# A decoder's product-key memory stage: masking in one operation, 1/Z on the one-hots, another order of work

## The reference

```python
q = (xn @ w_q.T).reshape(b, n, 2, h, kd).transpose(2, 0, 1, 3, 4)      # h = 8 heads
sim = jnp.einsum('pbnhd,hkpd->pbnhk', q, keys)                         # 2 sides x 8 heads x 32 keys
s, i = jax.lax.top_k(sim, k)                                           # k = 8
all_scores = (sx[..., :, None] + sy[..., None, :]).reshape(b, n, h, k * k)
scores, pk = jax.lax.top_k(all_scores, k)
w_down, w_up = key_in[idx], key_out[idx]                               # of 1024 experts
o = jnp.einsum('bnd,bnhkd->bnhk', inputs, w_down)
o = jax.nn.gelu(o, approximate=False) * jax.nn.softmax(scores, axis=-1)
return jnp.einsum('bnhk,bnhkd->bnd', o, w_up)
```

## Time and profile before

| | |
|---|---|
| median of 3 runs | 2909.44 us (2908.89 to 2909.66) |
| profiled execution | 2916.36 us, span 2914.3 us |
| TensorE busy | 2524.5 us (87%) |
| VectorE busy | 2382.4 us (82%) |
| ScalarE busy | 1835.6 us (63%) |
| GpSimd busy | 1101.8 us (38%) |
| mean granted TensorE clock | 0.926 of full speed |
| memory stage | from about 650 to 1433 us, 64 tiles |

### The profile page before, as it was taken

How to read it: one execution, slowest core, us unless ns; L and a number is a source line. 1 busy time by engine, 2 the same in 40 slices (tenths; PEclk the granted TensorE clock), 3 DMA queues, 4 the chain that set the end, 5 groups by cost and what they waited for, 6 DMA issues and landing times.

```text
span 2914.3 us, 95817 instructions
## 1 busy us (share of the span) xinstructions
PE 2524.5 (87%) x35786; PEld 1958.3 (67%) x35786; DVE 2382.4 (82%) x6431; ACT 1835.6 (63%) x3307; POOL 1101.8 (38%) x981
## 2 busy tenths in 40 slices
PE   2999963867888888888799999877789999999999
PEld 2666642546777777777566666555577888888887
DVE  6999989687899999999599999677767777777776
ACT  1777763544566666666366666565666777777776
POOL 1444420008899999999323232344413000000000
PEclk9999985977999999999799999798969999999999
DMA  5000000000000000000100000000001111111111
GB/s 165 1 0 0 0 15 0 1 0 2 1 0 0 0 0 0 0 0 0 59 1 0 0 0 0 9 15 16 14 5 52 51 55 51 54 51 54 55 53 48
DMA packets 47578, 60.44 MB, mean 21 GB/s; under 512 B 6672, under 2 KB 25872, under 8 KB 47376
## 3 DMA queue, kind: packets, MB, share of 16 engines
q1 hardware_dynamic: 47504, 59.45, 6.7%
HBM read 54.98 MB, written 4.46 MB: 20 GB/s over the span
## 4 chain that ended last, share of the span: by engine, by line
PE 77%; DVE 13%; issue 6%; DVEq 2%; ACT 1%; POOL 1%; DMA 0%; ACTq 0%; POOLq 0%; SPq 0%
PE ps L1064 8%; PE ps L885 8%; PE ps L1053 5%; PE ps L912 4%; PE ps L927 4%; PE ps L1078 4%; PE ps L1155 4%; PE ps L1133 4%; PE ps L1157 4%; PE ps L1156 4%; PE ps L1135 4%; PE ps L1134 4%; DVE work L1587 3%; DVE work L1636 2%; PE ps L940 2%
## 5 line engine op out<-in xcount | busy, mean ns | idle before, releaser
L479 POOL TENSOR_TENSOR work<-work,consts_sb 128x1024 f32<-128x1024 f32 x128 | 243.4, 1902 | 564.9 <-ACT work L603 564.9
L1064 PEld LDWEIGHTS ps<-work 32*32 32x32 f32 x16384 | 244.0, 145 | 126.7 <-issue 125.2
L1064 PE MATMUL ps<-work 32*32 32x32 f32 x16384 | 250.2, 226 | 76.0 <-DVE work L1587 60.8
L723 ACT ACTIVATE ps<-work 128x128 f32<-128x128 f32 x512 | 154.6, 354 | 233.6 <-DVE work L1569 222.6
L885 PE MATMUL ps<-work 128*128 128x512 f32 x512 | 262.5, 615 | 4.0 <-issue 2.8
L1730 DVE TENSOR_TENSOR h_low<-consts_sb,h_up 128x1024 fp32r<-128x1024 f32 x128 | 158.3, 1237 | 110.9 <-ACT h_up L794 110.8
L1133 PE MATMUL ps<-a_low,w_up 128*128 128x512 f32 x512 | 203.0, 396 | 0.9 <-DVE a_low L1705 0.9
L1155 PE MATMUL ps<-h_low,d_up 128*128 128x512 f32 x512 | 199.6, 390 | 2.3 <-DVE h_low L1730 2.3
L1730 DVE TENSOR_TENSOR h_low<-small_w,h_up 128x1024 fp32r<-128x1024 f32 x128 | 158.8, 1240 | 51.7 <-ACT h_up L794 51.7
L1135 PE MATMUL ps<-a_up,w_low 128*128 128x512 f32 x512 | 200.2, 391 | 0.0
L1134 PE MATMUL ps<-a_up,w_up 128*128 128x512 f32 x512 | 200.0, 391 | 0.0
(11 more groups left out here) (262 smaller groups left out, 6782.5 us busy)
## 6 DMA issues: line engine op xcount, KB each, us to landing
gates_spread<-gate_rows SPq DMA_DIRECT2D x128, 256.0 KB, 3.1
ctxT_all<-in_ctxT SPq DMA_DIRECT2D x1, 4096.0 KB, 12.9
work<-in_ctx SPq DMA_DIRECT2D x64, 64.0 KB, 1.8
out<-x_all SPq DMA_DIRECT2D x16, 256.0 KB, 3.5
big<-in_up SPq DMA_DIRECT2D x1, 2048.0 KB, 8.4
consts_sb<-in_consts SPq DMA_DIRECT2D x1, 936.0 KB
w<-in_key_inT SPq DMA_DIRECT2D x1, 512.0 KB, 3.4
w<-in_key_out SPq DMA_DIRECT2D x4, 128.0 KB, 3.8
```

The costliest lines, as they stand in the source:

```text
L1064: ins = pe.matmul(psW[rows, n // 16, :, n % 16], XT[rows, T.u, :, n], YT[rows, T.u, :, n], start=True, stop=True)
```

## The change

ScalarE's `shares` becomes `below_least`: the same eight operations into PSUM, but T8's eighth value minus the term, so that a term is chosen where the result is at most zero. VectorE's `chosen` becomes one operation over 1024 columns: (PSUM <= 0) times term. The factor 1/Z moves to the one-hots: GpSimd writes them into a block OH of their own (each one dense, 512 columns), and the new `scaled_one_hots` of ScalarE copies them, times 1/Z, into the strided places beside the terms, in eight operations of 128 columns. `turn_sides` waits for it, GpSimd's `ranks` too. The statistics of the sum are no longer behind a drain in `add_memory` but in `stats_with_memory`, a step later. The orders of ScalarE, TensorE and VectorE change: on TensorE mixed stands before hidden.

```diff
--- before.py
+++ after.py
@@ -240,7 +240,9 @@
         RZ = carve(2 * PH).rearrange("p (u h) -> p u h", u=2)
         IN2 = carve(2 * NS).rearrange("p (s h k) -> p s h k", s=2, h=PH)
         KI = carve(NEXP)
-        XY = carve(8 * NS).rearrange("p (k n h) -> p n h k", n=8, h=PH)
+        OH = carve(4 * NS).rearrange("p (r s h k) -> p s r h k", r=2, s=2, h=PH)
+        sides = carve(8 * NS)
+        XY = sides.rearrange("p (k n h) -> p n h k", n=8, h=PH)
         XT = carve(2 * NEXP).rearrange("p (u k t) -> p u k t", u=2, k=NKEY)
         YT = carve(2 * NEXP).rearrange("p (u k t) -> p u k t", u=2, k=NKEY)
         WT = carve(NEXP)
@@ -258,8 +260,8 @@
             return EX[:, u, BEST + NS:BEST + 5 * NS].rearrange("p (n h k) -> p n h k", n=4, h=PH)
 
         REST, DEEP_X, WIDE_Y = 0, 1, 3
-        chosen_terms = XY[:, 2:6]
-        one_hot = [XY[:, n:8:6] for n in range(2)]
+        chosen_terms = XY[:, 2:6].rearrange("p n h k -> p (n h) k")
+        one_hot_sides = sides.rearrange("p (k a r h) -> p a r h k", a=4, r=2, h=PH)[:, 0:4:3]
         x_side, y_side = [XY[:, n:n + 4].rearrange("p n h k -> p k (n h)") for n in (0, 4)]
 
         HC = HID // P
@@ -378,6 +380,7 @@
         rank_seen, keys_turned = sem("rank_seen"), sem("keys_turned")
         less_second, less_top, in2_ready, top_ready, hot_ready = (
             sem("less_second"), sem("less_top"), sem("in_top2_ready"), sem("top_ready"), sem("one_hot_ready"))
+        scaled_ready = sem("scaled_one_hots_ready")
         share_ready, xy_ready, sides_ready, spread_done, back_ready, back_turned = (
             sem("share_ready"), sem("xy_ready"), sem("sides_ready"), sem("spread_done"), sem("back_ready"), sem("back_turned"))
         h_done, h_ready, hg_ready, m_done = sem("h_done"), sem("h_ready"), sem("hg_ready"), sem("m_done")
@@ -526,14 +529,15 @@
             def ranks(T):
 
                 u = T.u
-                need(pool, sides_ready, T.before(1))
-                pool.tensor_tensor(one_hot[0], keys_of(u), best_of(u)[:, :, :, 0:1].to_broadcast([P, 2, PH, NKEY]), ALU.subtract)\
+                best, second = OH[:, :, 0], OH[:, :, 1]
+                need(pool, scaled_ready, T.before(1))
+                pool.tensor_tensor(best, keys_of(u), best_of(u)[:, :, :, 0:1].to_broadcast([P, 2, PH, NKEY]), ALU.subtract)\
                     .then_inc(less_top, 1)
                 pool.wait_ge(less_top, T.now())
                 pool.sem_inc(rank_seen, 1)
-                pool.tensor_scalar(one_hot[0], one_hot[0], 0.0, None, ALU.is_ge).then_inc(top_ready, 1)
+                pool.tensor_scalar(best, best, 0.0, None, ALU.is_ge).then_inc(top_ready, 1)
                 pool.wait_ge(top_ready, T.now())
-                pool.tensor_tensor(one_hot[1], IN2, one_hot[0], ALU.subtract).then_inc(hot_ready, 1)
+                pool.tensor_tensor(second, IN2, best, ALU.subtract).then_inc(hot_ready, 1)
             staggered(nc, pool, NT, [(0, candidates), (0, terms), (0, ranks)])
 
             pool.wait_ge(phase, PHASE["attn1"])
@@ -714,20 +718,31 @@
                 act.activation(first, first, ACT.Exp)
                 act.activation(y, y, ACT.Exp).then_inc(ex_ready, 1)
 
-            def shares(T):
-                u = T.u
-                act.wait_ge(rz_ready, T.now())
+            def below_least(T):
+
+                u = T.u
+                act.wait_ge(t8_ready, T.now())
                 act.wait_ge(terms_ready, T.now())
                 need(act, xy_ready, T.before(1))
                 for h in range(PH):
-                    ins = act.activation(psSH[:, :, h, :], terms_of(u)[:, :, h, :], ACT.Copy, scale=RZ[:, u, h:h + 1])
+                    ins = act.activation(psSH[:, :, h, :], terms_of(u)[:, :, h, :], ACT.Identity, scale=-1.0, bias=T8[:, u, h, TOPK - 1:TOPK])
                 ins.then_inc(share_ready, 1)
+
+            def scaled_one_hots(T):
+
+                u = T.u
+                act.wait_ge(hot_ready, T.now())
+                act.wait_ge(rz_ready, T.now())
+                need(act, sides_ready, T.before(1))
+                for h in range(PH):
+                    ins = act.activation(one_hot_sides[:, :, :, h, :], OH[:, :, :, h, :], ACT.Copy, scale=RZ[:, u, h:h + 1])
+                ins.then_inc(scaled_ready, 1)
 
             def hidden(T):
                 need(act, hg_ready, T.before(2))
                 act.wait_ge(h_done, T.now())
                 act.activation(HT[:, T.u], psH, ACT.Gelu).then_inc(h_ready, 1)
-            staggered(nc, act, NT, [(0, normed), (1, shares), (0, key_exps), (1, hidden)])
+            staggered(nc, act, NT, [(0, normed), (1, below_least), (0, key_exps), (1, scaled_one_hots), (1, hidden)])
 
 
             deviations(8)
@@ -1077,7 +1092,7 @@
                 for c in range(CHUNKS):
                     ins = pe.matmul(psM, HG[:, c, :], kout[:, c, :], start=c == 0, stop=c == CHUNKS - 1)
                 ins.then_inc(m_done, 1)
-            staggered(nc, pe, NT, [(0, key_scores), (2, spread_heads), (1, hidden), (3, mixed), (2, turn_weights)])
+            staggered(nc, pe, NT, [(0, key_scores), (2, spread_heads), (3, mixed), (1, hidden), (2, turn_weights)])
 
 
             b1 = ATTN["attn1"]
@@ -1572,16 +1587,15 @@
 
                 u = T.u
                 dve.wait_ge(share_ready, T.now())
-                for h in range(PH):
-                    ins = dve.scalar_tensor_tensor(out=chosen_terms[:, :, h, :], in0=terms_of(u)[:, :, h, :],
-                                                   scalar=T8[:, u, h, TOPK - 1:TOPK], in1=psSH[:, :, h, :],
-                                                   op0=ALU.is_ge, op1=ALU.mult)
-                ins.then_inc(xy_ready, 1)
+                need(dve, sides_ready, T.before(1))
+                dve.scalar_tensor_tensor(out=chosen_terms, in0=psSH.rearrange("p n h k -> p (n h) k"), scalar=0.0,
+                                         in1=terms_of(u).rearrange("p n h k -> p (n h) k"), op0=ALU.is_le, op1=ALU.mult)\
+                    .then_inc(xy_ready, 1)
 
             def turn_sides(T):
 
                 dve.wait_ge(xy_ready, T.now())
-                dve.wait_ge(hot_ready, T.now())
+                dve.wait_ge(scaled_ready, T.now())
                 need(dve, spread_done, T.before(2))
                 dve.transpose(XT[:, T.u], x_side)
                 dve.transpose(YT[:, T.u], y_side).then_inc(sides_ready, 1)
@@ -1601,9 +1615,13 @@
             def add_memory(T):
                 dve.wait_ge(m_done, T.now())
                 dve.tensor_tensor(xs[:, T.t, :], psM, xs[:, T.t, :], ALU.add).then_inc(y_used_m, 1)
-                stats_of_new(T)
-            staggered(nc, dve, NT, [(0, top_keys), (0, less_best), (1, chosen), (2, turn_back), (0, top_pairs), (3, add_memory),
-                                    (1, turn_sides), (0, pair_sums), (2, gated), (0, pair_shares)])
+
+            def stats_with_memory(T):
+                dve.wait_ge(y_used_m, T.now())
+                dve.sem_inc(x_seen, 1)
+                dve.bn_stats(st_all[:, T.t, :], xs[:, T.t, :])
+            staggered(nc, dve, NT, [(0, top_keys), (4, stats_with_memory), (0, less_best), (1, chosen), (2, turn_back), (0, top_pairs),
+                                    (0, pair_sums), (3, add_memory), (1, turn_sides), (0, pair_shares), (2, gated)])
```

## The result

The changed kernel takes 2939.8 us in the median of its runs (2929.3 to 2945.0), the kernel before 2909.7 beside it: ratio 1.0093, 95% interval 1.0069 to 1.0117. It is slower by 30 us; forecast were 33. The profiled execution of it took 2940.3 us with a span of 2938.3, against 2916.4 and 2914.3.

What follows compares the result with a forecast made beforehand. The kernel was taken as bound by a TensorE-VectorE ring of 11.14 us, then by one through ScalarE of 11.71. 0.52 us over 55 steps plus 5 us gave +33 us on 2909.4, so 2943 us, range 2915 to 2980.

Steps and rivals of the forecast that it cites:

- The ring: hidden, table load, gelu, normed, key_scores, spread_heads, mixed, next hidden: 11.71 us a step, from 11.2; chance 0.62.
- a fall of the clock: TensorE at half clock in the small matmuls; 0.82 us longer in about one step of three, striking mixed after the change.
- The sum: 55 steady periods x 0.52 = 28.6 us, plus 5 us for the 8 slower first steps: +33 us.
- The first steps: The stage's 8 slower first steps, same ring, key_scores at half clock in some: some 0.6 us each, 5 us.
- the dense row: Profile row for GpSimd's comparison of 512 columns: 2.448 us strided, 1.489 us dense, so 0.96 us less a step.
- ring (b): ScalarE and VectorE, through key_scores, less_best, statistics, key_exps, scaled_one_hots, load and gelu: 11.0 us, under 11.71.
- The drain: Rival: about 1380 ns added to each ScalarE table switch; 1.9 us for 63 steps, about 3030 us; chance 0.02.
- The first: Rival: gelu's table load runs ahead of the wait for hidden, ring 10.42 us, kernel faster at 2881 us; chance 0.16.
- ring (a): ScalarE and GpSimd, through terms, below_least, table load and key_exps: 10.7 us, under 11.71.
- more on top: Rival: clock falls in most steps, or scaled_one_hots costs over 4 us; 2972 us; chance 0.15.
- One sign that was named as right: Chain of waits shows ScalarE's table load, gelu and normed between hidden and key_scores in each step.
- a ring of 11.1 us: Old ring: spread_heads, hidden, mixed, VectorE's add_memory, drain, statistics, transposes; 11.14 us, falling to about 8.9 without hidden and drain.

Runs made afterwards that it cites:

- the old order: Changed kernel with TensorE's order of before, hidden ahead of mixed, all else as changed; against the kernel before: 2916.8 us, ratio 1.0018.
- longer GpSimd: Changed kernel with one more GpSimd operation of 128 columns inside terms, result unread; 2935.1 us, ratio 1.0083 to the kernel before.
- the new order and the early load: Kernel before with mixed ahead of hidden on TensorE and a one-column gelu ahead of ScalarE's waits for hidden; 2884.5 us, ratio 0.9914.
- the early load: Changed kernel with a one-column gelu ahead of ScalarE's waits for hidden, so the table load runs during the wait; 2857.8 us, ratio 0.9814.

## Why the prediction was right

**The ring.** Forecast 11.71 us without a fall of the clock; the short turns are 11.66. The pieces hold: 0.08, 1.30, 0.92, 0.61 (forecast 0.54), 1.05 (1.02), 3.80 (3.92), 1.95 (1.89), 1.95 (2.05). The mean was to be 11.71 + 0.82 / 3 = 11.98 and is 11.94. That the two means agree so well is luck, for the share of the clock in them is right by two errors. Every second turn takes 12.24 us, and what is slow in it is key_scores with 1.86 us (961.07) where mixed was expected. The clock falls in every turn now, behind TensorE's rest of 2 us. In one turn it falls as key_scores begins, and costs 0.57 us; in the next it falls in the small matmuls and costs nothing (TensorE in the changed kernel, the slow turn and the one after):

```profile
962.00:963.00 1.00, 1.00 (x11) 0.50 0.00 0
975.00:976.00 1.00, 1.00 (x85) 0.50 0.00 0
```

So the price is 0.57 us in one turn of two, where 0.82 in one of three was expected.

**The sum.** Steady periods: 55 x (11.94 - 11.46) = +26.5 us, forecast 28.6. The first steps, from the first normed to the steady part: 757.57 - 646.57 = 111.0 us against 755.76 - 650.75 = 105.0, +6.0, forecast +5. Not forecast: the end of the stage, from the last steady normed to the moments of the rows, is 6.3 us shorter (from there to the first operation of VectorE behind the stage, 1455.09 - 1414.49 against 1433.14 - 1386.20). The last steps have no normed and no key_scores, so the ring is open there; that this is where the 6.3 us come from is a reading that no run tested. Outside the stage 2.1 us came off. 26.5 + 6.0 - 6.3 - 2.1 is, but for rounding, the 24.0 us between the spans. The medians are 30 us apart; the runs of the changed kernel spread over 16 us.

**The engines.** The masking operation takes 1.957 us (taken: 1.8, between 1.21 and 2.24). GpSimd's comparison takes 1.487 in place of 2.448, as the dense row said. scaled_one_hots was over-priced: the eight take 2.55 us, not 3.3. A single one is 0.495 us long where one into PSUM (L723, before) is 0.354, but in both rows they start 0.29 us apart: the strided write lengthens each operation, and the next doesn't wait for that. With 2.55 ring (b) is 10.2 us. VectorE and GpSimd went down by 8% and 15%.

**The drain.** Load to gelu is 1.30 us again (970.55 to 971.85). The 1380 ns that the Trainium skill adds to a switch ("ScalarE: Activation LUTs", "What ACT_TABLE_LOAD costs") are in no turn here; with them the step could not be under 13 us.

**The rivals.** The first named the right lever: it said that with the load ahead of the wait the kernel would be faster, at 2881 us. The load was not ahead in the changed kernel, hence the forecast; put there by hand it gave 2857.8, because ring (a) came to 10.64 and the clock didn't fall any more; TensorE's rest ahead of key_scores shrank from 2.0 to 1.1 us a step (62.2 us in 58). Of "more on top" the first half came, falls of the clock in every turn, but at a price of 0.57 us in half of them. One sign that was named as right did not come: the chain of waits does not show the load between hidden and key_scores, for the reason above.

## What to carry to other kernels

Before an order of work is changed, follow each operation that is moved through every engine's queue round to itself, not only through the ring that the chain of waits shows: here hidden left a ring of 11.1 us and mixed entered another, which the chain of waits had not shown because it was 1.3 us shorter. Work that an engine could do while it waits, such as a table load, belongs ahead of the wait; one column of the function in front of it was worth 82 us. And a saving that shows no gain (27 us of the rest of the change here) may only be waiting for the ring to go.

## What the runs showed of the hardware

- A VectorE subtraction with both inputs in SBUF that starts 0.04 us or more into a GpSimd operation with two inputs in SBUF is held until 0.15 us after that one's end. In the old order it starts 0.04 to 0.38 us into it and takes 1.06 to 1.40 us in place of 0.27; in the changed kernel with longer GpSimd it starts 0.05 to 1.15 us into it and takes 0.29 to 1.39, and that kernel is not slower for it (2935.1 against 2939.8 us). In the old order more work on GpSimd made the kernel 34 us faster by moving the two apart. Beside GpSimd's strided comparison of 2.45 us, with one input, it took 0.29 to 0.56 us in the kernel before and 0.71 to 0.85 in 55 of 57 steps with the new order and the early load there, ending about 1.2 us before that one; beside the dense comparison 0.27 to 0.29. The Trainium skill ("GPSIMD Engine Reference", "Key points") says that GpSimd shares its SBUF interfaces with VectorE and contends with instructions of two SBUF inputs; the trace agrees and gives the size.
- A strided write, 256 bytes from one element to the next, costs VectorE 1.957 us for 1024 columns where another operation, of 1024 columns and dense, takes 1.21, but eight ScalarE operations of 128 such columns lose next to nothing (2.55 us against 2.41 into PSUM).
- The 256 small matmuls go at the same pace at half clock: 85 are under way in the microsecond from 975 at 0.50, and 88 in the one from 980 with the old order at 1.00. All 256 take 3.86 us in that turn and 3.85 with the early load at full clock. It is the dense group beside them that pays, and whether this is hidden's 16 passes (+1.6 us) or the 2 of key_scores (+0.7) depends on the order and on where TensorE rests.
